# Turning the probabilities of the first four query blocks in pairs, with half of the values copied to the upper partitions, in a Trainium2 decoder layer

## The chip, the cores and the metric

The kernel is one program written in Bass for one NeuronCore of a Trainium2 chip. The metric is the device time of one execution in microseconds (us), as the median of several runs; less is better.

## What is computed

A decoder layer of three parts, each followed by a layer norm without weights: attention, a mixture of experts, and a quantised linear layer. The input x has 16 sequences of 128 tokens of width 256. Cut to what matters here:

```python
# attention: 16 heads of 16
q, k, v = (heads(x @ W.T + b) for each)
scores = q @ k.T / 4, causal
keep the 32 largest scores of each query, softmax over them
out = probabilities @ v;  y = out @ Wo.T + bo
x = layernorm(x + y)
# 8 experts, all computed for all tokens, gated
x = layernorm(x + sum_e gate_e * (relu(x @ W1_e.T) @ W2_e.T))
# Hadamard, 4-bit activations, ternary weights
x = layernorm(x + ffn(x))
```

## The kernel before, in words

**Units and tiles.** The work goes in 8 units of two sequences (256 tokens). The attention of a unit is cut into 4 tiles: one sequence and 8 of the 16 heads each, so there are 32 tiles. Inside a tile the 128 queries are 8 blocks of 16; block j sees the first 16(j+1) keys. A tile has 128 partitions of (head, query in the block), and its blocks lie one behind the other in the free dimension.

**Steps of a tile.** TensorE computes the scores (L719) and adds the causal mask (L728); ScalarE copies them to SBUF (L549); VectorE finds the 32 largest by rounds of MAX8 and MATCH_REPLACE8 (L853 to L878); ScalarE takes exponentials (L563); VectorE multiplies by what is kept, which gives p_sb (`keep`, L887). In p_sb blocks 0 to 3 have 64 columns each and blocks 4 to 7 have 128 each (`prob_at`). Then `turn_probs` transposes p_sb on TensorE, one 128x128 transpose for a block (L739), in two halves of four blocks through the one PSUM bank ps_pt; `copy_probs` on ScalarE copies each half to pt_sb (L571), 64 rows for the first half, since its keys are 0 to 63. For blocks 0 to 3 the columns that are turned reach 64 columns into the next block, and these rows of the result are not used. The upper 64 rows of pt_sb for blocks 0 to 3 were set to zero once by GpSimd (L450) and stay zero.

**attend** (L749) multiplies probabilities by values: 8 heads times 4 strips of two blocks, 32 matmuls a tile. The stationary operand is 128 rows of keys by 32 columns (two blocks of 16 queries), the moving one is 17 columns of v_sb (16 of the head and a column of ones, which gives the sum for the softmax). Strip s writes partitions 32s to 32s+31 of ps_misc, so the four strips stand in four column strips of the array and follow each other in rotation. A float32 matmul is two passes, and the trace has two records for each. `normalise` on VectorE (L896, L898) divides into o_sb; when four tiles are done, `turn_o` (L679), `copy_ot` on ScalarE (two instructions, L580), `out_proj` (L671), the first layer norm and the experts (L776, L792) of the unit follow.

**Order of the work.** Each engine walks one list, SCHEDULE (L219), made from a table of due slots: 32 slots a unit, one for each half of an expert's layer. The tables STEADY, FIRST, SECOND and LAST (L102 to L141) give each step's slot, and the steps of an engine are sorted by it. The experts of one unit are thus interleaved with the attention tiles of the next. The values of a unit (`v`, `copy_v`, L543) are computed ahead, into a ring of 6. ps_misc is one PSUM bank which q, k, v, attend, turn_o, out_proj and others take in turn (`take_misc`). All DMAs are issued on the sync engine.

```python
for h in range(HG):                                  # attend
    for s, rows in enumerate(STRIPS):
        last = pe.matmul(ps_misc[rows, h * VW:(h + 1) * VW],
                         pt_sb[:, k % 2, h ^ SH * (s // 2), 2 * s:2 * s + 2, :]...,
                         v_sb[:, v % RING, b * HEADS + g * HG + h, :], start=True, stop=True)
```

Of the kernel before, what the change touches and what calls it, by code (L numbers as in the profile page):

```python
# [15 lines left out]
ACT = mybir.ActivationFunctionType  # L16
# [6 lines left out]
P = 128  # L23
BATCH, SEQ, D = 16, 128, 256
HEADS = 16
# [5 lines left out]
UB = 2  # L31
UT = UB * SEQ
UNITS = BATCH // UB
HG = P // DH
GROUPS = HEADS // HG
TILES = UB * GROUPS
QB = P // HG
BLOCKS = SEQ // QB
FREE_BLOCKS = TOPK // QB
HALF = BLOCKS // 2  # L40
STRIP = 32
STRIPS = [slice(i, i + STRIP) for i in range(0, P, STRIP)]
SH = STRIP // DH
VW = DH + 1
# [8 lines left out]
RING = 6  # L53
# [19 lines left out]
def prob_at(j):  # L73

    return 64 * j if j < HALF else 64 * HALF + P * (j - HALF)
# [7 lines left out]
ROUNDS = TOPK // 8  # L83
STAGES = 2 * ROUNDS - 1
# [7 lines left out]
def expert_steps():  # L92
# [9 lines left out]
STEADY = {  # L102
    "shift0": 1.25, "shift1": 0, "shift2": 1.75, "shift3": -1, "scores": -6.5, "copy_scores": -6.25, "exp": 5.5,
# [9 lines left out]
}  # L113
FIRST = STEADY | {
    "shift0": 2.5, "shift1": 1.25, "shift2": 0.5, "shift3": -0.25, "scores": -3, "copy_scores": -1.75, "select": 3,
# [41 lines left out]
    ("sp", "load_ctx"), ("sp", "load_x"), ("pool", "x_plus_bo"), ("pe", "turn_o"), ("act", "copy_ot"),  # L157
# [64 lines left out]
def decoder_layer(nc, x, xt, ctx_w, itok, wqt, bq, wkt, bk, wvt, bv, wot, bo, w1t, w2t, ffnt,  # L222
                  c_ident, c_hadamard, c_causal, c_heads, out):
    with ExitStack() as stack:  # L224
        def sb(name, shape, dt=F32):
            return stack.enter_context(nc.sbuf_tensor(name, shape, dt))

        def sem(name):
            return stack.enter_context(nc.semaphore(name))
# [6 lines left out]
        bq_sb, bk_sb, bv_sb = (sb(n, [P, CD]) for n in ("bq_sb", "bk_sb", "bv_sb"))  # L236
# [28 lines left out]
        v_sb = sb("v_sb", [P, RING, UB * HEADS, VW])  # L265
        s_sb = sb("s_sb", [P, 2, S_COLS])
# [5 lines left out]
        pt_sb = sb("pt_sb", [P, 2, HG, BLOCKS, QB])  # L272
        rsum = sb("rsum", [P, HG])
        o_sb = sb("o_sb", [P, UB, D])
        ot_sb = sb("ot_sb", [P, CD, UT])
# [40 lines left out]
        ps_pt, ps_misc = bank("ps_pt"), bank("ps_misc")  # L316
# [11 lines left out]
        s_xt, s_xa, s_x, s_ctx, s_store = sem("xt_loaded"), sem("xa_loaded"), sem("x_loaded"), sem("ctx_loaded"), sem("out_stored")  # L328
# [49 lines left out]
        def wait(eng, s, value):  # L378

            if value > 0:  # L380
                eng.wait_ge(s, value)
# [137 lines left out]
        def _(act):  # L519
# [4 lines left out]
            def step(name, v, *args):  # L524
# [41 lines left out]
                elif name == "copy_probs":  # L566
                    k, half = args
                    rows = P if half else P // 2
# [3 lines left out]
                        pt_sb[0:rows, k % 2, :, HALF * half:HALF * (half + 1), :].rearrange("p h j q -> p j h q"),  # L572
                        ps_pt[0:rows, :].rearrange("p (j h q) -> p j h q", h=HG, q=QB), ACT.Copy)\
                        .then_inc(pt_copied, 1)
                elif name == "copy_ot":
# [3 lines left out]
                    for c in range(CD):  # L579
                        last = act.activation(ot_sb[:, c, :], ps_misc[:, c * UT:(c + 1) * UT], ACT.Identity,  # L580
                                              bias=bv_sb[:, c:c + 1])
# [59 lines left out]
        def _(pe):  # L641
# [41 lines left out]
            def step(name, v, *args):  # L683
# [48 lines left out]
                elif name == "turn_probs":  # L732
# [4 lines left out]
                    for i in range(HALF):  # L737
                        at = prob_at(HALF * half + i)
                        last = pe.transpose(ps_pt[:, i * P:(i + 1) * P], p_sb[:, k % 2, at:at + P], ident[:, :])  # L739
                    last.then_inc(pt_ready, 1)  # L740
                elif name == "attend":
# [4 lines left out]
                    pe.wait_ge(v_copied, v + 1)  # L746
                    for h in range(HG):
                        for s, rows in enumerate(STRIPS):
                            last = pe.matmul(ps_misc[rows, h * VW:(h + 1) * VW],  # L749
                                             pt_sb[:, k % 2, h ^ SH * (s // 2), 2 * s:2 * s + 2, :]  # L750
                                             .rearrange("p j q -> p (j q)"),
                                             v_sb[:, v % RING, b * HEADS + g * HG + h, :], start=True, stop=True)
# [307 lines left out]
```

## Time and profile before

| what | value |
|---|---|
| median of 3 runs | 606.18 us (605.2 to 607.4) |
| the profiled execution | 605.08 us |
| its span, first to last instruction | 603.3 us |
| TensorE busy | 527.5 us, 87% |
| VectorE busy | 472.6 us, 78% |
| ScalarE busy | 385.9 us, 64% |
| GpSimd busy | 344.5 us, 57% |

Engines are named PE (TensorE matmul), PEld (TensorE weight load), DVE (VectorE), ACT (ScalarE), POOL (GpSimd) and SP (sync engine; SPq is its queue). L749 is line 749 of the kernel. A group is a set of instructions of one line, engine, operation and tile; "idle before" is the time that the engine was idle just before them, and what ended it. Ends of matmuls are modelled and overlap with the next, so what a matmul costs is read from start to start.

### The profile page before, as it was taken

How to read it: one execution, taken by the hardware profiler on the slowest of the kernel's cores; microseconds unless marked ns; L12 is line 12 of the kernel's file. 1: busy time of each engine (PE TensorE's matmuls, PEld its weight loads, DVE VectorE, ACT ScalarE, POOL GpSimd, SP SyncE). 2: the span in 40 equal slices, each digit the busy share in tenths (PEclk: the TensorE clock that was granted, in tenths of full speed). 3: DMA queues.
4: the chain of work that ended last, by engine and by line, in shares of the span. 5: the costliest groups of instructions: out<-in, count | busy, mean ns of one | idle time of the engine just before them, and what ended most of it. 6: DMA issues, size and time to landing. Idle time of an engine off the chain costs nothing. (4 is left out here: it accounts for less than half of the span.)

```text
span 603.3 us, 22386 instructions
## 1 busy us (share of the span) xinstructions
PE 527.5 (87%) x8180; PEld 450.2 (75%) x8180; DVE 472.6 (78%) x2995; ACT 385.9 (64%) x909; POOL 344.5 (57%) x336
## 2 busy tenths in 40 slices
PE   4567459999899999998999989998999999989941
PEld 3455347888778878887888878887888888878830
DVE  1777996968988998698899998999899999633213
ACT  2787765866667667675677657776686767555520
POOL 3447661875566646555375646665656556656831
PEclk9799767999999999999999999999999999999985
DMA  7253341010000010000100100010001000000000
GB/s 217 80 184 131 109 145 37 14 37 20 3 21 20 3 54 21 2 3 3 54 20 3 56 3 20 3 55 2 20 3 38 3 3 2 20 0 3 19 0 17
DMA packets 21933, 21.85 MB, mean 36 GB/s; under 512 B 1856, under 2 KB 19776, under 8 KB 21824
## 3 DMA queue, kind: packets, MB, share of 16 engines
q1 hardware_dynamic: 21824, 20.42, 10.8%
q8 instruction: 65, 1.06, 0.8%
q14 instruction: 44, 0.36, 0.2%
HBM read 18.32 MB, written 2.10 MB: 34 GB/s over the span
## 5 line engine op out<-in xcount | busy, mean ns | idle before, releaser
L478 POOL TENSOR_TENSOR h_lo<-h_raw,h_hi 128x512 f16<-128x512 f32 x128 | 148.7, 1164 | 126.8 <-ACT h_raw L598 125.8
L792 PE MATMUL ps_o<-w_hi,h_lo 128*128 128x256 f16 x512 | 139.8, 273 | 4.7 <-POOL h_lo L478 4.5
L776 PE MATMUL ps_z<-x1t_hi,w_lo 128*128 128x256 f16 x512 | 140.4, 274 | 0.7 <-DVE x1t_lo L934 0.7
L776 PE MATMUL ps_z<-x1t_lo,w_hi 128*128 128x256 f16 x512 | 140.2, 274 | 0.0
L776 PE MATMUL ps_z<-x1t_hi,w_hi 128*128 128x256 f16 x512 | 140.1, 274 | 0.0
L792 PE MATMUL ps_o<-w_lo,h_hi 128*128 128x256 f16 x512 | 139.6, 273 | 0.0
L792 PE MATMUL ps_o<-w_hi,h_hi 128*128 128x256 f16 x512 | 139.6, 273 | 0.0
L878 DVE MATCH_REPLACE8 taken<-next,taken 128x48 f32<-128x48 f32 (+2 forms) x576 | 127.4, 232 | 0.1
L594 ACT ACTIVATE h_hi<-ps_z 128x512 f16<-128x512 f32 x128 | 76.0, 594 | 70.5 <-PE ps_z L776 70.4
L499 POOL TENSOR_TENSOR acc<-go_sb,acc 128x512 f32<-128x512 f32 x56 | 71.4, 1276 | 58.9 <-ACT go_sb L608 58.1
L873 DVE MAX8 next<-taken 128x8 f32<-128x48 f32 (+2 forms) x576 | 95.7, 233 | 0.0
L598 ACT ACTIVATE h_raw<-ps_z 128x512 f32<-128x512 f32 x128 | 76.0, 594 | 0.0
L608 ACT ACTIVATE go_sb<-ps_o,gate 128x256 f32<-128x256 f32 x128 | 53.2, 467 | 17.0 <-PE ps_o L792 16.8
L571 ACT ACTIVATE pt_sb<-ps_pt 64x512 f32<-64x512 f32 x64 | 38.0, 594 | 39.2 <-PE ps_pt L739 39.2
L792 PEld LDWEIGHTS ps_o<-w_hi,h_lo 128*128 128x128 f16 x512 | 50.0, 98 | 13.8 <-POOL h_lo L478 6.8
L776 PEld LDWEIGHTS ps_z<-x1t_hi,w_lo 128*128 128x128 f16 x512 | 50.3, 98 | 8.1 <-DVE x1t_lo L934 0.9
L792 PEld LDWEIGHTS ps_o<-w_lo,h_hi 128*128 128x128 f16 x512 | 50.1, 98 | 6.9
L776 PEld LDWEIGHTS ps_z<-x1t_lo,w_hi 128*128 128x128 f16 x512 | 50.3, 98 | 6.0
L776 PEld LDWEIGHTS ps_z<-x1t_hi,w_hi 128*128 128x128 f16 x512 | 50.3, 98 | 6.0
L792 PEld LDWEIGHTS ps_o<-w_hi,h_hi 128*128 128x128 f16 x512 | 50.1, 98 | 5.8
L563 ACT ACTIVATE ps_s<-s_sb,neg_max 128x48 f32<-128x48 f32 (+2 forms) x192 | 51.5, 317 | 0.0
L853 DVE MAX8 top<-s_sb 128x8 f32<-128x16 f32 (+7 forms) x256 | 37.6, 218 | 13.6 <-ACT s_sb L549 13.5
(110 smaller groups left out, 950.3 us busy)
## 6 DMA issues: line engine op xcount, KB each, us to landing
w_raw<-in_w1t SPq DMA_DIRECT2D x8, 512.0 KB, 4.4
w_raw<-in_w2t SPq DMA_DIRECT2D x8, 512.0 KB, 5.5
xt_sb<-in_xt SPq DMA_DIRECT2D x8, 256.0 KB, 3.2
x_sb<-in_x SPq DMA_DIRECT2D x8, 256.0 KB, 2.9
out<-out_sb SPq DMA_DIRECT2D x8, 256.0 KB, 2.2
xa_sb<-in_xt SPq DMA_DIRECT2D x7, 256.0 KB, 3.1
ctx_sb<-in_ctx_w SPq DMA_DIRECT2D x8, 128.0 KB, 2.9
itok_sb<-in_itok SPq DMA_DIRECT2D x8, 128.0 KB, 3.0
```

The lines of the kernel that those rows point to most:

```text
L478: nc.gpsimd.tensor_tensor(h_lo[:, e % 2, 2 * z:2 * z + 2, :], h_raw[:, z, :, :], h_hi[:, e % 2, 2 * z:2 * z + 2, :], ALU.subtract)\
L499: nc.gpsimd.tensor_tensor(acc[:, :, :], go_sb[:, e % 2, :, :], prev[:, :, :], ALU.add)\
L563: last = act.activation(dst, s_sb[:, k % 2, score_at(j):score_at(j) + m], ACT.Exp, bias=neg_max[:, k % 2, j:j + 1], scale=SCALE)
L571: act.activation(pt_sb[0:rows, k % 2, :, HALF * half:HALF * (half + 1), :].rearrange("p h j q -> p j h q"), ps_pt[0:rows, :].rearrange("p ...
L594: act.activation(h_hi[:, e % 2, 2 * z:2 * z + 2, :], ps_z[z][:, :].rearrange("p (c t) -> p c t", c=2), ACT.Relu)\
L598: act.activation(h_raw[:, z, :, :], ps_z[z][:, :].rearrange("p (c t) -> p c t", c=2), ACT.Relu)\
L608: last = act.activation(go_sb[:, e % 2, b, :], ps_o[e % 2][:, b * D:(b + 1) * D], ACT.Copy, scale=gate[:, b, e:e + 1])
L776: last = pe.matmul(ps_z[z][:, d * UT:(d + 1) * UT], w[:, e, c, at:at + P], x[:, c, :], start=n == 0, stop=n == len(terms) - 1)
L792: last = pe.matmul(ps_o[e % 2][:, b * D:(b + 1) * D], h[:, e % 2, c, b * SEQ:(b + 1) * SEQ], w[:, e, c, :], start=n == 0, stop=n == len(te ...
L853: last = V.max(top8[:, k % 2, j, :], s_sb[:, k % 2, score_at(j):score_at(j) + QB * (j + 1)])
L873: last = V.max(next8[:, j, :], t)
L878: last = V.match_replace(t, next8[:, j, :], t, TAKEN)
```

## The change

Blocks 0 to 3 are turned in pairs: two transposes of 128 columns in place of four, so a tile has six. Block 2i then lies in the lower 64 partitions of ps_pt and block 2i+1 in the upper 64. `copy_probs` of the first half copies 128 rows by 256 columns. Since the probabilities of blocks 1 and 3 now stand in partitions 64 to 127, the values of keys 0 to 63 are needed there too: a new step `move_v`, once a unit, copies them with a DMA issued by ScalarE from SBUF to SBUF into v_low (two buffers; 64 partitions, 544 float32 each, 139 KB). `attend` still has 32 matmuls a tile, in another order and shape: first, for all 8 heads, strips 0 and 1 with 64 rows each (strip 0 rows 0 to 63, strip 1 rows 64 to 127), then, for all 8 heads, strips 2 and 3 with 128 rows. It has one more wait, for the DMA. The order of the blocks in o_sb is 0, 2, 1, 3, 4, 6, 5, 7, and `copy_ot` puts them back, with four instructions of 128 columns in place of two of 256. The tables name `move_v` twice each; the later entry counts (slot 2 of the unit, 8 in the first).

```diff
+PT_FROM, PT_COLS = (0, 2), (2, HALF)
+TURNED = (0, 2, 1, 3)
 STEADY = {
+    "move_v": -4,
+    "move_v": 2,
 FIRST = STEADY | {
+    "move_v": 6,
+    "move_v": 8,
-    ("sp", "load_ctx"), ("sp", "load_x"), ("pool", "x_plus_bo"), ("pe", "turn_o"), ("act", "copy_ot"),
+    ("sp", "load_ctx"), ("sp", "load_x"), ("act", "move_v"), ("pool", "x_plus_bo"), ("pe", "turn_o"), ("act", "copy_ot"),
+        v_low = sb("v_low", [P, 2, UB * HEADS, VW])
-        pt_sb = sb("pt_sb", [P, 2, HG, BLOCKS, QB])
+        pt_sb = sb("pt_sb", [P, 2, HG, sum(PT_COLS), QB])
                 elif name == "copy_probs":
                     k, half = args
-                    rows = P if half else P // 2
+                    at, cols = PT_FROM[half], PT_COLS[half]
                     act.wait_ge(pt_ready, 2 * n + half + 1)
                     wait(act, pv_ready, n - 1)
                     act.activation(
-                        pt_sb[0:rows, k % 2, :, HALF * half:HALF * (half + 1), :].rearrange("p h j q -> p j h q"),
-                        ps_pt[0:rows, :].rearrange("p (j h q) -> p j h q", h=HG, q=QB), ACT.Copy)\
+                        pt_sb[:, k % 2, :, at:at + cols, :].rearrange("p h j q -> p j h q"),
+                        ps_pt[:, 0:cols * P].rearrange("p (j h q) -> p j h q", h=HG, q=QB), ACT.Copy)\
                         .then_inc(pt_copied, 1)
+                elif name == "move_v":
+                    act.wait_ge(v_copied, v + 1)
+                    wait(act, pv_ready, TILES * (v - 1))
+                    act.dma_start(v_low[64:P, v % 2, :, :], v_sb[0:64, v % RING, :, :]).then_inc(s_low, 16)
                 elif name == "copy_ot":
...
                     for c in range(CD):
-                        last = act.activation(ot_sb[:, c, :], ps_misc[:, c * UT:(c + 1) * UT], ACT.Identity,
-                                              bias=bv_sb[:, c:c + 1])
+                        for r in range(2):
+                            last = act.activation(
+                                ot_sb[:, c, :].rearrange("p (f i r q) -> p f i r q", r=2, i=2, q=QB)[:, :, :, r, :],
+                                ps_misc[:, c * UT:(c + 1) * UT]
+                                .rearrange("p (f r i q) -> p f r i q", r=2, i=2, q=QB)[:, :, r, :, :],
+                                ACT.Identity, bias=bv_sb[:, c:c + 1])
...
                     pe.wait_ge(p_ready, n + 1)
                     wait(pe, pt_copied, 2 * n + half)
-                    for i in range(HALF):
-                        at = prob_at(HALF * half + i)
+                    for i in range(PT_COLS[half]):
+                        at = i * P if half == 0 else prob_at(HALF + TURNED[i])
                         last = pe.transpose(ps_pt[:, i * P:(i + 1) * P], p_sb[:, k % 2, at:at + P], ident[:, :])
...
                     pe.wait_ge(v_copied, v + 1)
+                    pe.wait_ge(s_low, 16 * (v + 1))
+                    heads = v_sb[:, v % RING, b * HEADS + g * HG:b * HEADS + (g + 1) * HG, :]
                     for h in range(HG):
-                        for s, rows in enumerate(STRIPS):
+                        low = v_low[64:P, v % 2, b * HEADS + g * HG + h, :]
+                        for on, rows, values in ((slice(0, 64), STRIPS[0], heads[0:64, h, :]),
+                                                 (slice(64, P), STRIPS[1], low)):
+                            pe.matmul(ps_misc[rows, h * VW:(h + 1) * VW],
+                                      pt_sb[on, k % 2, h, 0:2, :].rearrange("p j q -> p (j q)"), values,
+                                      start=True, stop=True)
+                    for h in range(HG):
+                        for rows, at in ((STRIPS[2], 2), (STRIPS[3], 4)):
                             last = pe.matmul(ps_misc[rows, h * VW:(h + 1) * VW],
-                                             pt_sb[:, k % 2, h ^ SH * (s // 2), 2 * s:2 * s + 2, :]
-                                             .rearrange("p j q -> p (j q)"),
-                                             v_sb[:, v % RING, b * HEADS + g * HG + h, :], start=True, stop=True)
+                                             pt_sb[:, k % 2, h ^ SH, at:at + 2, :].rearrange("p j q -> p (j q)"),
+                                             heads[:, h, :], start=True, stop=True)
                     last.then_inc(pv_ready, 1)
```

## Rows read from the trace of the kernel before

**Rows 1.** The page: busy time and instructions; then tenths of 40 slices.

```profile
PE 527.5 (87%) x8180; PEld 450.2 (75%) x8180; DVE 472.6 (78%) x2995; ACT 385.9 (64%) x909; POOL 344.5 (57%) x336
...
PE   4567459999899999998999989998999999989941
```

**Rows 2.** Stretches: length; busy of PE, PEld, DVE, ACT, POOL; clock; DMA share; GB/s.

```profile
32.40:90.00 57.60, 34.68 (x690) 27.14 (x694) 48.97 (x349) 43.28 (x93) 38.74 (x29) 0.80 0.41 134
...
336.00:398.00 62.00, 59.73 (x1006) 51.80 (x1005) 56.65 (x371) 42.14 (x106) 36.37 (x38) 1.00 0.07 20
...
520.00:603.30 83.30, 61.05 (x523) 51.52 (x521) 24.07 (x55) 33.31 (x68) 44.97 (x44) 0.88 0.03 10
```

**Rows 3.** What PE waited for from 90 to 520 us (total, times, longest).

```profile
PE ps_misc L679 <- DVE x L841: 8.1, 8, 1.7
PE ps_pt L739 <- DVE p_sb L887: 1.3, 3, 0.5
PE ps_pt L739 <- ACT pt_sb L571: 1.3, 1, 1.3
```

**Rows 4.** The group of attend's matmuls on PE, whole span.

```profile
L749 PE MATMUL ps_misc<-v_sb,pt_sb 128*32 128x17 f32 x2048 | 23.8, 187 | 0.7 <-ACT v_sb L543 0.7
```

**Rows 5.** PE in order of time around the first half of one turn_probs.

```profile
259.71 0.27 PE L792 MATMUL ps_o<-w_hi,h_hi 128*128 128x256 f16 x1
259.81 0.60 PE L739 MATMUL ps_pt<-ident,p_sb 128*128 128x128 f32 x4
260.25 0.27 PE L776 MATMUL ps_z<-x1t_hi,w_lo 128*128 128x256 f16 x1
```

**Rows 6.** PE and its weight loads in order of time around one attend.

```profile
244.14 0.27 PE L776 MATMUL ps_z<-x1t_hi,w_hi 128*128 128x256 f16 x1
244.34 0.64 PEld L749 LDWEIGHTS ps_misc<-v_sb,pt_sb 128*32 128x32 f32 x64 [0.21 <-issue]
244.34 0.74 PE L749 MATMUL ps_misc<-v_sb,pt_sb 128*32 128x17 f32 x64
245.01 0.28 PE L792 MATMUL ps_o<-w_hi,h_lo 128*128 128x256 f16 x1
```

**Rows 7.** Weight loads of that attend: ns min/median/max, and how many in its first stretch.

```profile
L749 PEld LDWEIGHTS ps_misc<-v_sb,pt_sb x64: 106/109/113, 244.3 to 244.9; 128*32 128x32 f32 x64
...
244.34:244.59 0.25, 0.25 (x33) 1.00 0.00 0
```

**Rows 8.** Two weight loads of 128 columns, one float32 matmul alone: time order; durations.

```profile
52.76 0.30 PEld L802 LDWEIGHTS ps_o<-w_sq,ones 128*128 128x128 f32 x2 [0.48 <-ACT w_hi L620]
...
L802 PEld LDWEIGHTS ps_o<-w_sq,ones x2: 186/188/189, 52.8 to 52.9; 128*128 128x128 f32 x2
```

**Rows 9.** Score matmuls in the first 0.15 us of a tile, 16 to 80 columns.

```profile
257.52:257.67 0.15, 0.14 (x24) 1.00 0.00 0
```

**Rows 10.** PE in order of time where attend follows the scores directly.

```profile
133.91 0.27 PE L728 MATMUL ps_s<-causal_h,ident_h 32*32 32x64 bf16 x4
134.11 0.74 PE L749 MATMUL ps_misc<-v_sb,pt_sb 128*32 128x17 f32 x64
```

**Rows 11.** copy_ot, the out_proj that waits for it, exponentials of 48 to 128 columns.

```profile
340.61 0.84 ACT L580 ACTIVATE ot_sb<-ps_misc,bv_sb 128x256 f32<-128x256 f32 x2 [0.66 <-PE ps_misc L679]
341.71 1.89 PE L671 MATMUL ps_misc<-wo_sb,ot_sb 128*128 128x256 f32 x8
...
343.71 1.61 ACT L563 ACTIVATE ps_s<-s_sb,neg_max 128x48 f32<-128x48 f32 x6
```

**Rows 12.** DMAs: issue of one on the sync engine; KB and us to landing.

```profile
401.57 0.47 SPq L396 DMA_DIRECT2D xt_sb<-in_xt  x1
...
itok_sb<-in_itok SPq DMA_DIRECT2D x8, 128.0 KB, 3.0
```

**Rows 13.** Around the third tile's turn in a steady unit, in order of time.

```profile
390.47 0.82 DVE L887 SCALAR_TENSOR_TENSOR p_sb<-taken,ps_s 128x640 f32<-128x640 f32 x1
...
391.34 0.66 PE L739 MATMUL ps_pt<-ident,p_sb 128*128 128x128 f32 x4 [0.43 <-DVE p_sb L887]
```

More of the change, by code:

```diff
@@ L327, in decoder_layer @@
                              "w_undo_step", "had_cast"))
-        s_xt, s_xa, s_x, s_ctx, s_store = sem("xt_loaded"), sem("xa_loaded"), sem("x_loaded"), sem("ctx_loaded"), sem("out_stored")
+        s_xt, s_xa, s_x, s_ctx, s_store, s_low = sem("xt_loaded"), sem("xa_loaded"), sem("x_loaded"), sem("ctx_loaded"), sem("out_stored"), sem("v_moved")
         zeroed, pool_const, cast_done, ffn_prep, ffn_abs, ffn_sum = (
```

## The prediction

> **What bounds the kernel now.** I read the page first: TensorE is busy 87% of the span, and eight or nine tenths or more in each slice from the seventh to the 36th; VectorE follows with 78% [rows 1]. Then the busy time by stretches. In the first tiles (32 to 90 us) TensorE works 35 of 58 us, since it waits for the weights' preparation; in a steady unit of 62.0 us it works 59.7, VectorE 56.7, ScalarE 42.1; after 520 us there are no tiles left [rows 2]. So 28 of the 32 tiles, those of units 1 to 7, lie where TensorE is the bound and VectorE comes close behind. Third, the waits of TensorE between 90 and 520 us: the largest is for the first layer norm, 8.1 us in all; ahead of the turns it is 1.3 us for p_sb and 1.3 us, once, for pt_sb [rows 3]. A microsecond of TensorE's own work in units 1 to 7 is thus a microsecond of the time, up to what those small waits take up.
>
> Next the group of attend: 2048 records of 187 ns, that is 64 passes in each of 32 tiles, yet only 23.8 us busy [rows 4]. The passes overlap, so what they cost is read from start to start in time order.
>
> **Part 1, the turns (a gain).** Four transposes start at 259.81 and the next matmul at 260.25: 0.44 us, 0.11 us each, and they follow the expert matmul of 259.71 with no gap [rows 5]. Two fewer a tile save 0.22 us. ScalarE's copy of the first half goes from 64x512 to 128x256; TensorE waited for such a copy once in 28 tiles [rows 3], so I cost that saving at nothing: the expert matmuls between turn and attend hide the copy, and at most that 1.3 us could come back.
>
> **Part 2, attend (the term that decides).** Now: the last expert matmul before attend starts at 244.14, and would be followed after 0.11 us; attend starts at 244.34, so 0.09 us go in the change of shape; the next expert matmul starts at 245.01, 0.67 us later [rows 6]. Inside, the 64 weight loads span 0.64 us of which the last is 0.11, so they start within 0.53 us, 8.4 ns apart; in the first 0.25 us there are 33 of them, 7.8 ns apart. One load takes 106 to 113 ns from its start to its end [rows 6, 7].
>
> What sets 8 ns? The four strips rotate, so one strip gets a pass every 31 to 34 ns. A float32 load of 128 columns on one and the same strip of columns is followed by the next after 0.30 - 0.19 = 0.11 us, though only 2 columns stream through [rows 8]: 0.86 ns per column, or 27 ns for 32 columns. That is nearly the 31 to 34 ns of a strip. And it is not the issue of instructions: in the scores, where 32x32 tiles give more places in rotation, 24 passes start in 0.14 to 0.15 us, 6 ns apart, although they stream more columns (16 to 80, against 17) [rows 9]. So I read attend as bound by the successive weight loads of each strip, four strips side by side.
>
> After the change only two strips are in rotation at a time: 32 passes on strips 0 and 1, then 32 on strips 2 and 3. Each strip still has 16 passes of about 32 ns, so each block takes 16 x 32 = 0.51 us, and both 1.02 us against 0.53: +0.49 us a tile. Using 64 rows in place of 128 shortens nothing, since the load goes by columns. Between the blocks the shape changes from 64 to 128 rows. From 32x32 to 128x32, where only the rows change, the four last mask matmuls start at 133.91, the last about 0.07 later, and attend at 134.11 [rows 10]: about 0.13 us with the mask matmul's own 0.03, so again some 0.09 us. I take +0.09 for the added change of shape. The added semaphore wait is taken while earlier matmuls still run: nothing.
>
> Sum of a tile on TensorE: -0.22 + 0.49 + 0.09 = **+0.36 us**. Over 28 tiles: +10.1 us. In unit 0 TensorE is idle for two fifths of the time [rows 2], so both saving and cost go into its idle time: 0.
>
> **Part 3, what waits absorb.** In the third tile of a steady unit the turns wait 0.43 us for p_sb, which VectorE makes from 390.47 on [rows 13]; ahead of it in VectorE's list stand `gate_sums`, which need nothing of TensorE. A TensorE that is later by 0.36 us loses that much of this wait. All such waits between 90 and 520 us come to 1.3 us [rows 3], and I take all of it: -1.3 us. The waits for the layer norm stay, since their chain starts from TensorE's own out_proj.
>
> **Part 4, copy_ot.** Two instructions of 256 columns take 0.84 us. No row has 128 columns in this form; the nearest are six exponentials of 48 to 128 columns in 1.61 us, 0.27 each [rows 11]. Four of those take 1.1 us and a little for the last one's end, some 1.16: +0.32 us. out_proj starts at 341.71, 0.26 us after copy_ot's end at 341.45 [rows 11]. So 0.06 us come through, seven times: +0.4 us. From below: nothing, if four fit into 1.1; from above, if each costs as much as one of 256 columns (0.42), +0.84 - 0.26 = 0.58 a unit, 4.1 us. I take the value by the exponentials, which are nearest in columns.
>
> **Part 5, move_v.** The DMA is issued on ScalarE's queue eight times. No row has a DMA there; the nearest is one on the sync engine, 0.47 us [rows 12]. ScalarE is idle a third of a unit, so between 0 and 8 x 0.47 = 3.8 us; I take 0.6, near the lower end, as ScalarE mostly waits for TensorE itself. Behind it in ScalarE's list are copies of experts' results and the exponentials; TensorE waits for the first through two banks ps_z. Landing: 128 KB take 3.0 us [rows 12]; the step stands at slot 2 and the first attend of the unit past slot 12, at 62/32 = 1.9 us a slot about 20 us later; in unit 0 it stands at slot 8 and the first attend past slot 14, some 12 us at the same pace. Hidden in both, and if that cover were gone, 3 us a unit. Its own wait for earlier attends is for those of two units before, long done. Sync's and GpSimd's queues get nothing new.
>
> **The sum.** 10.1 - 1.3 + 0.4 + 0.6 = +9.8 us on the profiled execution's 605.1, that is 614.9; the median of the runs stands 1.1 us above that execution, so 616.0 us; I round down by half a microsecond, since unit 0 may keep some of its saving: **615.5 us**.
>
> **The rivals.**
>
> *A. The strips overlap after all (faster).* If passes of strips 2 and 3 start while those of 0 and 1 still run (they use other columns and other PSUM partitions), or if what sets 8 ns is a load path that all strips share, attend keeps its 0.53 us. Place: L749's block, 64 passes between two expert matmuls; it decides when the added cost falls below 0.22 us a tile. For it: the hardware does reorder, as the scores' 6 ns shows more than one tile at work. Against it: each change of shape in the trace shows 0.09 us of emptiness [rows 6, 10], which an overlap would not leave. Price: -0.22 + 0.09 = -0.13 x 28 = -3.6 us, 602.6; without the added 0.09, -6.2 us, 600.0, of which VectorE, close behind, may take back 1 or 2. I give 0.14.
>
> *B. Half of it.* The first block's tail is overlapped by the second, so a tile costs -0.22 + 0.25 = about +0.03: +1 us, 606 to 608. Chance 0.06.
>
> *C. Weight loads go by rows.* If a load overlapped only with work in other rows, the two halves of the first block would now run side by side, which they did not before: before, 64 loads of 27 ns one after the other would make 1.7 us, after it 0.43 + 0.86 = 1.3 us, -0.4 a tile; with the turns -0.6 x 28 = -18 us, 588. The trace of before speaks against it: 64 loads start in 0.53 us, all on the same 128 rows [rows 6, 7]. Chance 0.03. The Trainium skill has this rule (TensorE: Matmul & The Clock Gate, Part 3, What overlaps and what doesn't: weight loads overlap with matmuls in flight only when the row group differs); this trace does not agree with it, by those 0.53 us.
>
> *D. The copy is late or ScalarE is held.* The transfer's 3.0 us lie open in each of 8 units: +24 us over the forecast, 639. Place: attend's new wait. Against it: the cover of part 5. Chance 0.02.
>
> **How the numbers follow.** Forecast (attend bound by its strips): 0.75, its own range 610 to 620: low with a strip's round at 31 ns and one more wait absorbed a unit, high with 34 ns (0.63 - 0.22 = 0.41 a tile, 11.5 us), or copy_ot's or the DMA issue's upper end. Rivals as above. The range reaches down to part of A: 601.5 to 620. About 0.3% (1.8 us) is what a measurement of this kernel can tell from no change. Faster by more than that: A and C, 0.17; within it: B mostly, 0.05; slower: 0.78.
>
> **What would show it.** In the trace after: attend from its first pass to the next expert matmul near 1.2 us in place of 0.67, with a gap of about 0.09 us between the passes of 64 rows and those of 128, and starts 16 ns apart; two transposes of the first half in 0.22 us; copy_ot near 1.1 us; no wait of TensorE for the DMA; a unit of about 63.3 us in place of 62.0. It is wrong if the passes start 8 ns apart with two strips (rival A), or if the unit grows though attend doesn't (D).

## The result, and the profile after

The change makes the kernel slower: 617.25 us (median of 4 runs, 615.41 to 617.95) against 606.37 us (4 runs of the kernel before beside it). The ratio is 1.0174, interval 1.0152 to 1.0196: +10.9 us, where 615.5 us was forecast. The profiled execution took 617.73 us.

First the page of the changed kernel: the span, the busy time, and the DMA queue that is new.

```profile
span 615.9 us, 22320 instructions
PE 541.1 (88%) x8116; PEld 462.0 (75%) x8116; DVE 475.1 (77%) x2995; ACT 383.6 (62%) x925; POOL 344.6 (56%) x336
...
q10 hardware_dynamic: 640, 1.11, 0.8%
```

TensorE has 64 instructions fewer (two transposes in each of 32 tiles) and 13.6 us more busy time than in [rows 1]. ScalarE and GpSimd are busy for no longer than before; VectorE's busy time grew by 2.5 us, though it has the same 2995 instructions. The granted clock is 1.00 in both kernels over the whole stretch from 100 to 580 us, so TensorE's clock has no part in the difference there. Next the same steady unit as the second of [rows 2], in the view of stretches:

```profile
342.00:406.20 64.20, 61.21 (x998) 53.06 (x997) 57.65 (x371) 41.91 (x107) 36.44 (x38) 1.00 0.07 21
```

The unit grew from 62.0 to 64.2 us, more than the 63.3 that was forecast: the growth sits in the steady units, but a second cost must lie beside attend's. It isn't the same in all units: from first attend to first attend, units 2 and 3 grew by 1.1 and 1.2 us, units 4, 5 and 6 by 2.3, 2.2 and 2.1. Now TensorE in order of time around one attend, the counterpart of [rows 6]:

```profile
247.55 0.27 PE L799 MATMUL ps_z<-x1t_hi,w_hi 128*128 128x256 f16 x1
247.75 0.20 PE L768 MATMUL ps_misc<-v_sb,pt_sb 64*32 64x17 f32 x1
247.76 0.20 PE L768 MATMUL ps_misc<-v_low,pt_sb 64*32 64x17 f32 x1
...
248.25 0.18 PE L768 MATMUL ps_misc<-v_sb,pt_sb 64*32 64x17 f32 x1
248.26 0.18 PE L768 MATMUL ps_misc<-v_low,pt_sb 64*32 64x17 f32 x1
248.37 0.69 PE L773 MATMUL ps_misc<-v_sb,pt_sb 128*32 128x17 f32 x32
248.99 0.28 PE L815 MATMUL ps_o<-w_hi,h_lo 128*128 128x256 f16 x1
```

The passes of the two strips start as a pair, some 7 ns apart, and the next pair follows 25 ns later: 32 ns for one strip. After the last pass of 64 rows there is nothing for 110 ns, then the block of 128 rows starts. From the expert matmul before attend to the one behind it: 1.44 us here, 0.87 in [rows 6]. Over all steady tiles the median is 1.433 against 0.872, +0.561 us.

The waits of TensorE, the counterpart of [rows 3], moved with the tiles to 92 to 532 us (total, times, longest):

```profile
PE ps_misc L694 <- DVE x L864: 7.9, 8, 1.7
PE ps_pt L754 <- DVE p_sb L910: 3.5, 3, 1.2
PE ps_misc L686 <- DVE x2t_lo L957: 1.5, 6, 0.3
PE ps_pt L754 <- ACT pt_sb L578: 1.1, 1, 1.1
```

The wait for the layer norm is the old one. The wait for p_sb was to vanish; it went from 1.3 to 3.5 us, 1.2 us each time. A wait for GpSimd's h_lo that the view of before lists beside [rows 3] is gone:

```profile
PE ps_o L792 <- POOL h_lo L478: 2.0, 6, 0.4
```

The one for x2t_lo, which VectorE makes for the third part of the layer, is new. Here is one of its six, in the changed kernel:

```profile
305.81 0.69 DVE L957 TENSOR_TENSOR x2t_lo<-ps_misc,x2t_hi 128x512 f16<-128x512 f32 x1 [1.44 <-ACT x2t_hi L602]
...
306.60 0.27 PE L686 MATMUL ps_misc<-had_h,x2t_lo 128*128 128x256 f16 x1 [0.28 <-DVE x2t_lo L957]
```

The two transposes that fell away stand 1.6 us ahead of this matmul, and it starts not a moment sooner for it: 0.10 us behind the end of x2t_lo, as in the kernel before, with 0.22 us more of idle time in front (in five of the six, less in the last). In these tiles, one a unit, the saving of the turns is given back at once.

Here is one turn that waits, with VectorE and GpSimd around it, in order of time. First the kernel before, whose p_sb and turn stand in [rows 13]:

```profile
373.06 0.21 DVE L896 RECIPROCAL rsum<-ps_misc 128x8 f32<-128x8 f32 x1 [0.55 <-PE ps_misc L749]
...
390.25 0.29 DVE L919 SCALAR_TENSOR_TENSOR gate_part<-itok_sb,ctx_sb 128x128 bf16<-128x128 int32 x1
390.33 1.34 POOL L499 TENSOR_TENSOR acc<-go_sb,acc 128x512 f32<-128x512 f32 x1 [1.77 <-ACT go_sb L608]
```

Then the changed kernel:

```profile
380.56 0.21 DVE L919 RECIPROCAL rsum<-ps_misc 128x8 f32<-128x8 f32 x1 [1.10 <-PE ps_misc L773]
...
397.55 0.28 DVE L942 SCALAR_TENSOR_TENSOR gate_part<-itok_sb,ctx_sb 128x128 bf16<-128x128 int32 x1
397.61 1.35 POOL L506 TENSOR_TENSOR acc<-go_sb,acc 128x512 f32<-128x512 f32 x1 [1.77 <-ACT go_sb L623]
397.76 1.34 DVE L942 SCALAR_TENSOR_TENSOR gate_part<-itok_sb,ctx_sb 128x128 bf16<-128x128 int32 x1
399.04 0.81 DVE L910 SCALAR_TENSOR_TENSOR p_sb<-taken,ps_s 128x640 f32<-128x640 f32 x1
399.90 0.44 PE L754 MATMUL ps_pt<-ident,p_sb 128*128 128x128 f32 x2 [1.15 <-DVE p_sb L910]
```

This is the turn of the last tile of a unit (the prediction called it the third). VectorE is released by an attend, computes rsum, and then works until p_sb, with the same 1.0 us of idle time in all in both kernels: 17.41 us before, 18.48 after. The 1.07 us are one gate sum. A gate sum takes 0.28 us; the last of the eight started 0.15 us after GpSimd's gated add and lasted until 0.14 us behind its end, 1.34 us in all. Before, the last gate sum started 0.08 us *ahead* of the add, and took 0.29. The add hangs on TensorE: it starts 17.27 us after that rsum before, and 17.05 after, 0.22 us earlier. That is the time of the two transposes that fell away in between. So the saving itself brings the add in front of the last gate sum. The same step of 1.06 to 1.07 us stands at the last tile of units 4, 5 and 6, and in no other steady tile. That the gate sum is held, and not merely slowed, shows in the others: in the kernel before, 11 of the 128 gate sums last over 0.4 us. They begin between 0.04 and 1.24 us into an instruction of GpSimd, and every one ends 0.14 to 0.15 us behind the end of that instruction. The Trainium skill names the resource (GPSIMD Engine Reference, 1. Specifications): GpSimd's SBUF interfaces are shared with VectorE, with contention when a VectorE instruction has two SBUF inputs. The rows agree: the gate sum, with itok_sb and ctx_sb, stalls; p_sb, with one input in PSUM, takes 0.81 us beside an add and without one.

Last, copy_ot and out_proj, the counterpart of [rows 11]:

```profile
347.30 1.14 ACT L592 ACTIVATE ot_sb<-ps_misc,bv_sb 128x128 f32<-128x128 f32 x4 [0.66 <-PE ps_misc L694]
348.30 0.27 PE L799 MATMUL ps_z<-x1t_hi,w_hi 128*128 128x256 f16 x1
348.58 0.45 PE L686 MATMUL ps_misc<-wo_sb,ot_sb 128*128 128x256 f32 x1
```

copy_ot takes 1.14 us, ends at 348.44, and out_proj starts 0.14 us later. The matmul ahead of it started at 348.30, so TensorE lost 348.58 - 348.41 = about 0.18 us. From out_proj's first start to the next expert matmul it is 1.80 us in place of 1.73, another 0.07. Both stand at six of the eight out_proj, those of units 2 to 7; the ones of units 0 and 1 start as before. And the new DMA: duration of its issue on ScalarE's queue, and its way to landing.

```profile
L585 ACTq DMA_DIRECT2D v_low<-v_sb x8: 468/469/507, 25.0 to 470.1; - x8
...
DMA to landing us min/median/max: 2.2/2.9/3.3
```

No wait of TensorE ends with it.

### The profile page after: what moved, and what is told of

The parts are those of the page before. It is cut to its first block and busy times, and to the rows that moved or that the text cites. A ratio compares the mean times of both kernels' runs of the same rounds, so it can differ in the third digit from the quotient of the medians.

```text
span 615.9 us, 22320 instructions
## 1 busy us (share of the span) xinstructions
PE 541.1 (88%) x8116; PEld 462.0 (75%) x8116; DVE 475.1 (77%) x2995; ACT 383.6 (62%) x925; POOL 344.6 (56%) x336
## 3 DMA queue, kind: packets, MB, share of 16 engines
q8 instruction: 65, 1.06, 0.7%
## 5 line engine op out<-in xcount | busy, mean ns | idle before, releaser
L815 PEld LDWEIGHTS ps_o<-w_hi,h_lo 128*128 128x128 f16 x512 | 50.0, 98 | 10.9 <-POOL h_lo L485 3.2
L578 ACT ACTIVATE pt_sb<-ps_pt 128x256 f32<-128x256 f32 x64 | 31.6, 493 | 41.1 <-PE ps_pt L754 40.1
L876 DVE MAX8 top<-s_sb 128x8 f32<-128x16 f32 (+7 forms) x256 | 37.6, 218 | 14.8 <-ACT s_sb L556 14.6
```

The source lines that it names most:

```text
L578: act.activation(pt_sb[:, k % 2, :, at:at + cols, :].rearrange("p h j q -> p j h q"), ps_pt[:, 0:cols * P].rearrange("p (j h q) -> p j h q ...
L815: last = pe.matmul(ps_o[e % 2][:, b * D:(b + 1) * D], h[:, e % 2, c, b * SEQ:(b + 1) * SEQ], w[:, e, c, :], start=n == 0, stop=n == len(te ...
L876: last = V.max(top8[:, k % 2, j, :], s_sb[:, k % 2, score_at(j):score_at(j) + QB * (j + 1)])
```

## The experiments

Twelve kernels ran, in three groups; each group has its own runs of the kernel before. Ratios are to those.

### 1. Two strips in rotation, rows unchanged (`b_two_strips`)

The kernel before, with attend's loop in two groups of strips and nothing else changed:

```diff
+                    for group in ((0, 1), (2, 3)):
                         for h in range(HG):
-                            for s, rows in enumerate(STRIPS):
+                            for s in group:
```

> The kernel before, with attend alone changed: its 64 passes come in two groups, strips 0 and 1 for all heads, then strips 2 and 3, all with 128 rows as before; nothing is left out and nothing else moves. Theory (each strip takes a pass every 31.7 ns, so two in rotation halve the rate): attend goes from 0.554 us first to last start to 32 x 31.7 ns = about 1.0 us with no gap in the middle, +0.46 us a tile, over 28 tiles +13 us, 619 us. Rival (a shared load path or the issue of instructions sets 8 ns a pass): attend stays 0.55 us and the time within 1 us of before, 606.

Measured: 612.06 us against 606.05, ratio 1.009 (1.0057 to 1.0122). TensorE in order of time around an attend:

```profile
245.49 0.27 PE L777 MATMUL ps_z<-x1t_hi,w_hi 128*128 128x256 f16 x1
245.69 1.10 PE L750 MATMUL ps_misc<-v_sb,pt_sb 128*32 128x17 f32 x64
246.72 0.28 PE L793 MATMUL ps_o<-w_hi,h_lo 128*128 128x256 f16 x1
```

From expert to expert 1.23 us, +0.36 a tile. The order of the same 64 instructions costs that: the bound is per strip, as part 2 said. The time lies midway between theory (619) and rival (606), since both hold in part. It is less than the 0.49 of part 2, since in the middle the passes of strips 2 and 3 start while those of 0 and 1 are still under way: the 64 passes start within 0.916 us from first to last, not 1.02. Rival A was right to that extent, where no shape changes in between. And +0.36 x 28 = 10.1 us of TensorE's time became only 6.0 us of the kernel's: what the waits list between 93 and 524 us fell from 14.6 to 10.4 us.

### 2. The same groups, the first with 64 rows (`b_two_strips_64`)

As 1, but strips 0 and 1 use rows 0 to 63 alone, both the same rows (keys 64 to 127 of the first four blocks are left out):

```diff
+                                on = slice(0, 64) if s < 2 else slice(0, P)
```

> As the run in two groups with 128 rows, but strips 0 and 1 use rows 0 to 63 alone, both of them, so that the shape changes once inside attend. Theory: +0.09 us for the change of shape on top of 1.0 us, attend 1.11 us as in the changed kernel, about +2.5 us against the run with 128 rows, 621 us. Rival 1 (rows matter: loads of the same row group do not overlap, those of different ones do): strips 0 and 1, now on the same rows, would run one after the other, attend well above the changed kernel's 1.115 us. Rival 2 (64 rows load faster): the first group shorter than the second.

Measured: 616.15 us, ratio 1.0159 (1.0127 to 1.0191), where 621 was expected; attend is as expected.

```profile
249.34 1.30 PE L751 MATMUL ps_misc<-v_sb,pt_sb 64*32 64x17 f32 x64
250.57 0.28 PE L794 MATMUL ps_o<-w_hi,h_lo 128*128 128x256 f16 x1
```

The attend of this kernel is that of the change: 1.115 us from the first start to the last, pairs 7 and 25 ns apart, a gap of 110 ns. It does not matter whether two strips side by side load from the same 64 rows (here) or from different halves (the change). That settles rival C. The Trainium skill has weight loads overlap with matmuls in flight only when the row group differs (TensorE: Matmul & The Clock Gate, Part 3, What overlaps and what doesn't); this run does not agree, by its pairs 7 ns apart on the same 64 rows. Against experiment 1 the change of shape costs 1.115 - 0.916 = 0.2 us: 0.1 for the gap, and 0.1 because it forbids the overlap in the middle.

### 3. Six turns without the new attend (`b_six_turns`)

The kernel before, with blocks 2 and 3 neither turned nor copied; a constant stands for their probabilities in attend, whose 64 passes are as before.

```diff
-                    for i in range(HALF):
+                    for i in range(HALF if half else 2):
```

> The kernel before with two of the eight transposes of a tile left out: blocks 2 and 3 are not turned nor copied, and attend multiplies a constant in their place. It measures the saving of the turns alone. Theory (TensorE's own work bounds units 1 to 7): 28 x 0.218 = 6.1 us less, 600.3 us. Rival (VectorE is the real bound close behind): the wait for p_sb grows by what TensorE gains, and the time falls by 2 to 3 us only, 603.5.

Measured: 608.69 us, ratio 1.0038 (1.0019 to 1.0057): slower, with 28 x 0.218 = 6.1 us less work on TensorE. A clear miss, and the most useful run. Its waits from 93 to 520 us, and one last tile in order of time:

```profile
PE ps_misc L680 <- DVE x L842: 9.4, 9, 2.1
PE ps_pt L740 <- DVE p_sb L888: 5.3, 4, 1.7
PE ps_o L793 <- POOL h_lo L478: 2.0, 6, 0.4
PE ps_misc L672 <- DVE x2t_lo L935: 1.5, 6, 0.3
```

```profile
376.83 0.21 DVE L897 RECIPROCAL rsum<-ps_misc 128x8 f32<-128x8 f32 x1 [0.55 <-PE ps_misc L750]
...
393.82 0.28 DVE L920 SCALAR_TENSOR_TENSOR gate_part<-itok_sb,ctx_sb 128x128 bf16<-128x128 int32 x1
393.88 1.34 POOL L499 TENSOR_TENSOR acc<-go_sb,acc 128x512 f32<-128x512 f32 x1 [1.77 <-ACT go_sb L609]
394.03 1.34 DVE L920 SCALAR_TENSOR_TENSOR gate_part<-itok_sb,ctx_sb 128x128 bf16<-128x128 int32 x1
395.30 0.81 DVE L888 SCALAR_TENSOR_TENSOR p_sb<-taken,ps_s 128x640 f32<-128x640 f32 x1
```

The same picture as in the change: the add 17.05 us behind the rsum, the last gate sum 0.15 us behind the add, stalled. In this tile TensorE idles 1.88 us ahead of the turn, counted from when its last matmul would have been followed (the view, which counts from the modelled end, has 1.71): the 0.60 of before, 0.22 that it is earlier, and 1.06 of the stall. In experiment 1, with eight turns, the add is 17.27 us behind the rsum and the last gate sum, 0.07 us ahead of it, takes its 0.29 us: nothing stalls.

This run has one more cost, and it stands in no view of waits. TensorE waits 2.08 us for the layer norm's x (1.46 in the kernel before), and behind that wait the granted clock is half for 3.4 us. The wait, and the stretch in the columns of [rows 2], with a clock of 0.50:

```profile
222.95 1.09 PE L680 MATMUL ps_misc<-ident,x 128*128 128x128 f32 x4 [2.08 <-DVE x L842]
```

```profile
222.95:226.30 3.35, 3.35 (x16) 2.74 (x17) 3.35 (x30) 1.58 (x4) 0.62 (x1) 0.50 0.02 5
```

The expert matmuls start 0.21 us apart there in place of 0.11. From the first matmul behind this wait to the twelfth expert matmul the stretch takes 3.53 us, against 2.10 before, two transposes included: with their 0.22 us that is 1.65 us lost to the clock. Of the ten executions only this one is profiled, so how many of them had the drop isn't known; their mean clocks run from 0.941, this one's, to 0.950.

### 4. The change with four strips in rotation (`a_four_strips`)

The values of strip 0 and of strip 1 lie in two buffers of 128 partitions, one half zeros, filled by two DMAs a unit at slot 5; attend has one shape and four strips in turn:

```diff
-                    for h in range(HG):
-                        low = v_low[64:P, v % 2, b * HEADS + g * HG + h, :]
...
+                    for h in range(HG):
+                        m = b * HEADS + g * HG + h
+                        for rows, at, x, values in ((STRIPS[0], 0, h, v_up[:, m, :]),
+                                                    (STRIPS[1], 0, h, v_low[:, m, :]),
+                                                    (STRIPS[2], 2, h ^ SH, v_sb[:, v % RING, m, :]),
+                                                    (STRIPS[3], 4, h ^ SH, v_sb[:, v % RING, m, :])):
```

> The changed kernel with attend in the old shape: all passes with 128 rows and the four strips in rotation. Strips 0 and 1 take the same turned pair and multiply it by values padded with zeros, in the lower or in the upper 64 rows, so two copies by DMA a unit, single buffers, at slot 5. Six turns, copy_ot and the rest as in the change. Theory: attend back at 0.554 us, 28 x 0.56 = 15.7 us less than the changed kernel's 617.3, so 601.6 us, less than before by 4 to 5 us; the second DMA on ScalarE costs up to 1 us of it. Rival (the DMA, copy_ot or VectorE's stalls carry the loss): the time stays above 610 us.

Measured: 608.88 us, ratio 1.0045 (1.0027 to 1.0062). attend is back at 0.554 us from first to last start, and the kernel is some 8 us faster than the change, so attend's form is where most of the added time was. The 601.6 expected is missed all the same: it isn't faster than the kernel before, though TensorE is busy 3.5 us less. One last tile shows why:

```profile
391.75 1.34 POOL L508 TENSOR_TENSOR acc<-go_sb,acc 128x512 f32<-128x512 f32 x1 [1.77 <-ACT go_sb L628]
391.90 1.35 DVE L943 SCALAR_TENSOR_TENSOR gate_part<-itok_sb,ctx_sb 128x128 bf16<-128x128 int32 x1
...
394.04 0.44 PE L759 MATMUL ps_pt<-ident,p_sb 128*128 128x128 f32 x2 [1.72 <-DVE p_sb L911]
```

Again 0.15 us, again the stall. The stretch from the rsum to this turn, in six kernels (last tiles of units 4 to 6, which agree to 0.02 us; the idle time is counted from start to start, as above):

```text
kernel             turns  add behind rsum  rsum to p_sb  rsum to turn  TensorE idles
before             8      17.27            17.41         18.28         0.60
b_two_strips       8      17.27            17.41         18.28         0.24
b_two_strips_64    8      17.27            17.41         18.29         0.04
b_six_turns        6      17.05            18.48         19.34         1.88
a_four_strips      6      17.05            18.48         19.34         1.88
the change         6      17.05            18.48         19.34         1.32
```

In this tile VectorE sets the pace. TensorE's work may grow by 0.56 us or shrink by 0.22, and the stretch doesn't move; what moves it is the stalled gate sum. Whole traces say the same. b_two_strips_64 has the change's attend, eight turns and the old copy_ot; experiment 12 below has that attend and copy_ot too, and six turns. From the fifth attend to the last its trace is 0.4 us longer, with 5.9 us less of turning.

### 5 to 8. The gate sums later (`b_gates`, `b_six_gates`, `a_gates`, `a_four_gates`)

If the gate sums ahead of p_sb are the trouble, they might be moved: one due time, in the kernel before, in 3, in the change and in 4.

```diff
-    "x_plus_bo": 15.75, "gate_sums": 30,
+    "x_plus_bo": 15.75, "gate_sums": 31.5,
```

> The kernel before with one number changed: gate_sums of the steady units (2 to 6) at slot 31.5 in place of 30, that is behind the third attention tile's keep and normalise in VectorE's list, as in units 0, 1 and 7. Theory (the turns of that tile wait because VectorE has eight or more gate sums ahead of p_sb): the waits of 0.25 to 0.6 us a unit go, 2.3 us less in all, 603.8 us. Rival (the wait is for something else, or VectorE's later work then comes late): within 1 us of before.

> The kernel before with two of eight transposes left out (blocks 2 and 3 are neither turned nor copied, a constant stands for them) and gate_sums at slot 31.5. Theory (the saving of the turns was lost in the run before in stalls of VectorE: a gate sum that starts beside GpSimd's gated add lasts 1.35 us in place of 0.28, ahead of keep, in units 4 to 6 and more): with gate_sums behind keep the saving appears, 5 to 6 us less than the same kernel with all turns, about 598 us. Rival (TensorE isn't the bound of these units, so fewer turns bring nothing): 602 to 604 us, no less than the kernel with all turns.

> The changed kernel with gate_sums of the steady units at slot 31.5. Theory: the turns' wait of 1.32 us in units 3 (1.34), 4, 5 and 6 goes, 4 to 5 us less than the changed kernel, 612.5 us; what stays over before is attend's 28 x 0.34 less what else is absorbed. Rival (the wait only moves to the next step that needs VectorE): 616 to 617 us.

> Four strips in rotation with padded values, six turns, and gate_sums at slot 31.5. Theory: 1.88 us of wait a unit go in four units and 0.3 in two, about 8 us less than the 608.9 of the same kernel with gate_sums at slot 30: 601 us, less than before. Rival: VectorE is late elsewhere, 605 to 608 us.

Measured, against 605.73: 626.0 (1.0336, 1.0307 to 1.0364), 623.77 (1.0313, 1.028 to 1.0347), 627.38 (1.036, 1.0335 to 1.0384) and 625.75 (1.0358, 1.0318 to 1.0398). All four miss. The wait for p_sb did go, in all of them, and a larger one came, for o_sb; that for x is the old one, 9.2 us here and 8.1 before. The waits of TensorE from 100 to 530 us in `b_gates`, the group of its gate sums, and a stretch that begins within the first of the new waits:

```profile
PE ps_misc L679 <- DVE o_sb L898: 15.5, 5, 3.9
PE ps_misc L679 <- DVE x L841: 9.2, 8, 1.7
```

```profile
L919 DVE SCALAR_TENSOR_TENSOR gate_part<-itok_sb,ctx_sb 128x128 bf16<-128x128 int32 x128 | 49.8, 453 | 0.0
```

```profile
213.45:220.20 6.75, 5.13 (x20) 4.08 (x21) 5.62 (x41) 2.98 (x9) 1.55 (x2) 0.50 0.40 118
```

The gate sums now stand ahead of the normalisation that turn_o needs, and meet more of GpSimd's work: 453 ns each on average. In the kernel before it is 339:

```profile
L919 DVE SCALAR_TENSOR_TENSOR gate_part<-itok_sb,ctx_sb 128x128 bf16<-128x128 int32 x128 | 35.4, 339 | 0.0
```

And the granted clock falls to half in some of the new waits and stays there behind them: for 17.1 us in all in `b_gates` between 110 and 580 us, where it is full throughout in the kernel before. Of the 22.1 us that the trace grew from the fifth attend to the last, about 16 are the waits for o_sb, and 6.6 stand in matmuls of experts and of out_proj whose starts have moved apart at half the clock. In the other three kernels the stretches at half come to 13.7, 3.4 and 13.7 us. With these costs in each of the four kernels, they can't say what six turns are worth without the stall.

### 9 to 11. Only `keep` ahead of them (`b_keep_first`, `b_six_keep_first`, `a_four_keep_first`)

A smaller step: 30.5, by which the instruction that makes p_sb passes eight gate sums.

```diff
-    "x_plus_bo": 15.75, "gate_sums": 30,
+    "x_plus_bo": 15.75, "gate_sums": 30.5,
```

> The kernel before with gate_sums of units 2 to 6 at slot 30.5: in VectorE's list only keep (p_sb of the third tile) and the first eight gate sums change places, everything else stays where it is. It is the control for the same swap in two other kernels. Theory (eight gate sums, 1.7 us, stand ahead of p_sb and the turns wait for it): the turns' wait of 0.25 to 0.6 us in these units goes and no other comes, 604 us. Rival (the run with slot 31.5 showed that these sums collide with GpSimd wherever they stand): the sums now start beside the gated add, last 1.3 us and delay normalise and turn_o, 608 us or more.

> Two of eight transposes left out (blocks 2 and 3 neither turned nor copied, a constant in their place), and the swap of keep and the gate sums. Theory: the 1.88 us of wait for p_sb in units 3 to 6 go, and the saving of the turns appears: 3 to 5 us less than the kernel with all turns and the same swap, 600 us. Rival (TensorE does not bound these units; VectorE and its stalls do): no less than 604 us.

> Four strips in rotation with padded values, six turns, and the swap of keep and the gate sums. Theory: the same 5 to 8 us under the 608.9 of this kernel without the swap, 602 us, which would be less than before. Rival: as above, 607 us or more.

Measured, against 606.57: 627.15 (1.0351, 1.0329 to 1.0372), 629.87 (1.0393, 1.0376 to 1.041) and 626.24 (1.032, 1.029 to 1.0349). Misses for the same reasons; in `b_keep_first` the waits for o_sb come to 16.0 us over the span, the longest 3.8, and 6.8 us of the steady units run at half the clock (23.9 and 17.1 us in the other two). One of its gate sums:

```profile
207.76 1.27 POOL L499 TENSOR_TENSOR acc<-go_sb,acc 128x512 f32<-128x512 f32 x1
...
207.82 1.36 DVE L919 SCALAR_TENSOR_TENSOR gate_part<-itok_sb,ctx_sb 128x128 bf16<-128x128 int32 x1
```

p_sb follows its rsum by 16.47 us instead of 17.41, so the stretch above is shorter and no turn waits. The eight gate sums behind it then run beside GpSimd and delay what comes next: 24 of 128 last over 0.4 us, against 11 before. I had counted what the step leaves and not what it moves into.

### 12. copy_ot in two instructions (`a_plain_ot`)

The change, with copy_ot as before (ot_sb's columns then stand in the order of the paired blocks):

```diff
-                        for r in range(2):
...
+                        last = act.activation(ot_sb[:, c, :], ps_misc[:, c * UT:(c + 1) * UT], ACT.Identity,
+                                              bias=bv_sb[:, c:c + 1])
```

> The changed kernel with copy_ot as before, two instructions of 256 columns; it leaves out that the blocks are put back in order. Theory (copy_ot's four instructions last 1.14 us in place of 0.84 and out_proj starts 0.18 us late in each unit): 7 x 0.18 = 1.3 us less than the change, 616 us. Rival (ScalarE has slack there): no difference, 617.3 us.

Measured: 615.41 us (613.6 to 620.26), ratio 1.0166 (1.0136 to 1.0197) to 606.57. copy_ot is back at 0.84 us:

```profile
344.66 0.84 ACT L591 ACTIVATE ot_sb<-ps_misc,bv_sb 128x256 f32<-128x256 f32 x2 [0.66 <-PE ps_misc L690]
```

TensorE's 0.18 us ahead of out_proj are gone, and the 0.07 behind. From the fifth attend to the last the trace is 1.6 us shorter than that of the change, of which 5 x 0.25 = 1.25 us is this. The intervals of the two ratios overlap: the traces show this size, the times don't.

## Why the prediction came out

The direction and the mechanism of the main term were right, and its size to within half a microsecond; of the smaller terms two were not, and one had the wrong sign. That their sum still came out near is in part luck, as below.

**Part 1, the turns** (-0.22 a tile): right on TensorE, 0.218 measured. That a microsecond of TensorE's work is a microsecond of the time was too simple. It fails in the tile whose turn is followed by the wait for x2t_lo, where all 0.22 us are given back. It fails in the last tile of a unit too, where VectorE sets the pace, and there the saving has a price of its own, below. Experiment 3, which has this part alone, is 2.6 us slower than the kernel before where 6.1 us of work was saved.

**Part 2, attend** (+0.49 and +0.09): measured +0.561 a tile, 0.02 less than the sum. A strip takes a pass every 31.7 ns, whatever the rows (experiments 1 and 2), and the shape change leaves 110 ns. Together with part 1 TensorE's work grew by 0.343 a tile, 9.6 us over 28 tiles, where 10.1 was the term.

**Part 3, what waits absorb** (-1.3): the step that failed. TensorE was later, and in the last tiles of units 4 to 6 it did give up 0.34 us of the wait for p_sb; but p_sb itself became later by 1.06 us, in units 4, 5 and 6. The idle time ahead of the last turns of units 2 to 6 went from 0.25, 0.25, 0.62, 0.60, 0.60 to 0, 0, 1.34, 1.31, 1.32 us: +1.65 us. I had looked at how late TensorE is against VectorE, and not at how early GpSimd's add comes against VectorE's gate sums, 0.08 us from a stall of 1.06. Where a later TensorE did absorb its own delay was a wait that the prediction doesn't name, that for h_lo: it is gone, and counted from start to start that is 0.49 us, six times, -2.9 us.

**Part 4, copy_ot** (+0.4): 1.14 us against the 1.16 expected, but 0.25 us came through in each of six units, 1.5 us in all: 0.18 ahead of out_proj and 0.07 in it. The mis-sized part is the slack: I took all of the 0.26 us from the copy's end to out_proj as free, and 0.14 of it is still there when TensorE waits for the copy. What the 0.07 are is not shown; they are gone when copy_ot has two instructions (experiment 12).

**Part 5, move_v** (+0.6): issue 0.47 us and landing 2.9 us as taken; no wait of TensorE could be seen, so nothing.

**The sum.** From the fifth attend to the last the trace grew by 10.5 us. There are 27 attends and 27 turns in it, 9.3 us of work; 1.3 us are left, where parts 3 to 5 together had -0.3. Laid side by side with the kernel before, start by start, they are: the turns of the last tiles, +1.6; the wait for x2t_lo, +1.1; out_proj, 5 x 0.25 = +1.2; smaller steps at the first expert matmuls of a unit and at the layer norm, +0.8; and against them h_lo, -2.9, and other waits, -0.3. That makes +1.5, 0.2 more than there is. So the forecast stood within 2 us of the result in part because a gain of 2.9 us and losses of some 3 us that it didn't have cancelled. The whole span grew by 12.6: 2.0 us of it are there before the first attend, at the weights' preparation, 0.7 go back before the fifth, and 0.8 come behind the start of the last attend, that attend's own 0.56 among them. The stretch before the first attend moved between -0.9 and +3.3 us from one kernel to another, in kernels that differ from the one before only in attend too, so I don't count it to the change; what moves it is open. The medians differ by 10.9 us.

**The rivals.** A holds where the shape stays the same (experiment 1, 0.13 of the 0.49 us a tile) and not in the change. B did not occur: a tile costs 0.34 us more, not 0.03. C is refuted by experiment 2. D did not occur. The rival that the prediction lacked is "TensorE gets earlier and nothing is gained", and experiments 3 and 4 show it. That the clock and not the waits carries the added time is excluded for the change, whose steady units ran at 1.00, and holds in part for experiments 3 and 5 to 11.

**What stays open.** That the stalled gate sum costs 1.06 us in its tile is read from the traces, in three kernels with six turns and three with eight, to 0.02 us. That the order of the add and the last gate sum is what decides it fits all six, but no run moves that order alone. That without it six turns would bring their 0.22 a tile was to be shown by experiments 5 to 11, and was not: they took the stall from one place to others, and the clock fell with it. Experiments 3 and 4 are better accounted for. Between the fifth attend and the last their traces grew by 3.1 and 2.8 us. The listed waits come to 21.1 us in both, 6.5 more than before, and the turns save 5.9: +0.6. In experiment 3 the clock adds 1.65 us; experiment 4 keeps the change's copy_ot, +1.2. Less than 1 us is left in each, in small steps. No version found beats the kernel before.

## What to carry to other kernels

Before shortening one engine's work, follow the path in each stretch: where two engines run neck and neck, look at which instruction releases which, and by how much they miss a conflict; here 0.08 us of distance decided over 1.06 us. When a kernel is slower than its waits explain, look at the granted clock stretch by stretch. Small matmuls packed into column strips are priced by the busiest strip: count passes per strip, keep all strips in rotation, and keep one shape. A new order of instructions has to be costed at the place that it moves to as well as at the one that it leaves.

## What was not expected of the hardware

- A VectorE scalar_tensor_tensor with two SBUF inputs, 0.28 us alone, that starts 0.15 us into GpSimd's tensor_tensor of 128x512 lasts until 0.14 us behind its end, 1.34 us; one that starts 0.06 us ahead of it takes its 0.28. It isn't slowed in proportion, it is held: the 11 long ones of the kernel before all ended 0.14 to 0.15 us behind GpSimd's instruction, wherever in it they began.
- Passes of the next pair of strips start while the last pair's still run if the shape is the same (0.916 us for 64 passes in two groups), and 110 ns later if the rows change from 64 to 128 (1.115 us).
- The first matmul behind a ScalarE copy that it waits for started 0.14 us after the copy's end.
- At the end of a wait of TensorE of 2.08 us the granted clock fell from 1.00 to 0.50 for 3.4 us (b_six_turns), and within one of 3.9 us for 6.8 us (b_gates). The half clock cost 1.65 us in the first case, and no view of waits shows it.
